# The first layer's key mask and key bias, added by VectorE and GpSimd instead of by row products on TensorE

## What is computed

```python
xn = _ln(x, ln_w, ln_b)
q = xn @ Wq + bq
k = xn @ Wk + bk + (1.0 - src_mask) * -1000000.0
q = softmax(q.reshape(b, t, h, dh), axis=-1)
k = softmax(k.reshape(b, t, h, dh), axis=1)      # over the 128 tokens
v = ((xn @ Wv + bv) * src_mask).reshape(b, t, h, dh)
att = einsum('bnhd,bnhl->bhdl', k, v)
y = einsum('bnhd,bhdl->bnhl', q, att).reshape(b, t, d)
scale, shift = split(silu(emb) @ W_emb + b_emb, 2)
hh = _ln(y, ln2_w, ln2_b) * (1.0 + scale) + shift
x = x + silu(hh) @ W_out + b_out
```

## Time and profile before

| | us |
|---|---|
| median of 3 runs | 2030.45 |
| the profiled execution | 2030.41 |
| its span, first to last instruction | 2028.6 |
| TensorE busy (granted clock 0.998) | 2002.7, 99% |
| VectorE busy | 1369.9, 68% |
| ScalarE busy | 1139.7, 56% |
| GpSimd busy | 573.2, 28% |
| one pair of layer 0, from 509.26 to the next pair's first key matmul at 537.75 | 28.49 |

### The profile page before, as it was taken

One profiled execution on the slowest core, in us unless ns is written; L12 is line 12 of the kernel. 1 busy time (PEld: TensorE's weight loads), 2 busy tenths in 40 slices (PEclk: granted clock), 3 DMA queues, 4 the chain that ended last, 5 costly groups with the idle time before them and its releaser, 6 DMA issues.

```text
span 2028.6 us, 52150 instructions
## 1 busy us (share of the span) xinstructions
PE 2002.7 (99%) x19499; PEld 1732.0 (85%) x19499; DVE 1369.9 (68%) x2995; ACT 1139.7 (56%) x3806; POOL 573.2 (28%) x861
## 2 busy tenths in 40 slices
PE   7999999999999999999999999999999999999997
PEld 5888888888888888888888888888888888888886
DVE  6877777777777777776666666666565656666665
ACT  4333343234333343244677777777777777777775
POOL 4233332333233332335222222222222222222220
PEclk9999999999999999999999999999999999999999
DMA  6311001110111001102110110101010101011000
GB/s 224 113 41 41 29 33 41 41 37 30 36 41 41 31 31 41 41 33 86 56 37 27 36 41 21 42 26 37 26 37 26 37 26 37 28 35 41 21 32 22
DMA packets 52165, 86.45 MB, mean 43 GB/s; under 512 B 5667, under 2 KB 14565, under 8 KB 52134
## 3 DMA queue, kind: packets, MB, share of 16 engines
q1 hardware_dynamic: 52118, 86.03, 12.5%
q10 hardware_dynamic: 16, 0.00, 0.0%
HBM read 52.32 MB, written 33.69 MB: 42 GB/s over the span
## 4 chain that ended last, share of the span: by engine, by line
PE 96%; DVE 2%; ACT 1%; DMA 0%; issue 0%; SPq 0%; POOL 0%; POOLq 0%; DVEq 0%; ACTq 0%
PE bank L538 16%; PE bank L540 14%; PE bank L539 14%; PE bank L547 9%; PE bank L548 9%; PE bank L549 9%; PE bank L559 7%; PE bank L1812 3%; PE bank L1787 3%; PE bank L1150 3%; PE bank L1136 2%; PE bank L1744 2%; PE bank L1781 1%; PE bank L1822 1%; PE bank L1038 1%; PE bank L1067 1%
## 5 line engine op out<-in xcount | busy, mean ns | idle before, releaser
L547 PE MATMUL bank<-xT_hi,w_hi 128*128 128x256 f32 x1536 | 448.9, 292 | 2.1 <-DVE xT_lo L379 1.4
L548 PE MATMUL bank<-xT_lo,w_hi 128*128 128x256 f32 x1536 | 438.8, 286 | 0.0
L549 PE MATMUL bank<-xT_hi,w_lo 128*128 128x256 f32 x1536 | 435.7, 284 | 0.0
L1598 ACT ACTIVATE heads<-bank,top 128x128 f32<-128x128 f32 x1024 | 359.2, 403 | 88.1 <-DVE top L1381 87.9
L538 PE MATMUL bank<-w_hi,xT_hi 128*128 128x512 f32 x768 | 306.3, 399 | 0.4 <-DVE bias_all L396 0.4
L547 PEld LDWEIGHTS bank<-xT_hi,w_hi 128*128 128x128 f32 x1536 | 291.9, 190 | 10.8 <-issue 5.1
L540 PE MATMUL bank<-w_lo,xT_hi 128*128 128x512 f32 x768 | 301.1, 392 | 0.0
L539 PE MATMUL bank<-w_hi,xT_lo 128*128 128x512 f32 x768 | 300.2, 391 | 0.0
L952 ACT ACTIVATE heads<-bank,k_neg 128x128 f32<-128x128 f32 x256 | 69.9, 377 | 404.4 <-DVE k_neg L814 404.4
L548 PEld LDWEIGHTS bank<-xT_lo,w_hi 128*128 128x128 f32 x1536 | 292.7, 191 | 0.5 <-issue 0.5
L549 PEld LDWEIGHTS bank<-xT_hi,w_lo 128*128 128x128 f32 x1536 | 292.9, 191 | 0.0
(11 more groups left out here) (204 smaller groups left out, 3730.8 us busy)
## 6 DMA issues: line engine op xcount, KB each, us to landing
xr<-in_x SPq DMA_DIRECT2D x32, 512.0 KB, 3.4
x_between_layers<-ends SPq DMA_DIRECT2D x64, 256.0 KB, 2.0
xr<-x_between_layers SPq DMA_DIRECT2D x32, 512.0 KB, 4.1
out<-ends SPq DMA_DIRECT2D x64, 256.0 KB, 2.1
store<-in_L_cond_W_emb SPq DMA_DIRECT2D x4, 1024.0 KB, 11.8
store<-in_L_cond_emb_w SPq DMA_DIRECT2D x3, 1024.0 KB, 8.2
mask_rows<-mask_parts SPq DMA_DIRECT2D x128, 2.0 KB
heads<-in_L_cond_Wk SPq DMA_DIRECT2D x1, 1024.0 KB, 7.8
```

What stands on the lines that cost most here:

```text
L547: yield nc.tensor.matmul(dst, w_hi[:, m, c, fs], a_hi[:, c], start=(first and c == 0), stop=False)
L548: yield nc.tensor.matmul(dst, w_hi[:, m, c, fs], a_lo[:, c], start=False, stop=False)
L549: yield nc.tensor.matmul(dst, w_lo[:, m, c, fs], a_hi[:, c], start=False, stop=(last and c == C - 1))
L1598: last = nc.scalar.activation(prob[:, a, c, :], ps[a][:, c * P:(c + 1) * P], ACT.Exp, bias=top[:, b, h:h + 1], accum_out=total[:, b, h:h + 1])
```

## The change

The mask (already times -1000000, less its largest value) is no longer split into parts for layer 0. It is written to memory and read back once per pair as a tile `key_mask` of 128 equal partitions, one slot, one pair ahead. VectorE adds it to the key block and takes the maximum in one operation per block of 128 x 128, with the sum written to `k_exp` and the maximum to `k_max`; each such operation is built as two instructions, the operation and a read of the accumulator. The key bias is left out of the exponent altogether, since it is constant along the tokens: GpSimd adds it to the maximum (`k_top`) and subtracts that from the bias (`k_neg`), and ScalarE takes the exponential of `k_exp` in place with `k_neg`. The bias is now four columns (`key_bias_cols`), made in the opening by four narrow matmuls and one addition. TensorE's row products are gone, and with them the tiles of rows, their four memsets and ScalarE's four small loads.

```diff
@@ first_steps, sync
+        sp.wait_ge(mask_step, 4)
+        sp.dma_start(mask_d[0, 0], mask_in[:, 0, :]).then_inc(mask_out, 16)
         sp.wait_ge(mask_step, 6)
         for n, part in enumerate((mask_hi, mask_lo)):
-            sp.dma_start(mask_d[:, n].rearrange("l b t -> b l t"), f32(part)).then_inc(mask_out, 16)
+            sp.dma_start(mask_d[1, n], f32(part[:, 1, :])).then_inc(parts_out, 16)
+        sp.wait_ge(mask_out, 16)
+        load_key_mask(sp, m, mask_d, 0, s["masks_in"])
         sp.wait_ge(x_in, 16)
         load_rows(sp, x_d, m.xr, 1, 1, x_in)
         emb.load(sp, range(4))
-        sp.wait_ge(mask_out, 32)
+        sp.wait_ge(parts_out, 32)
@@ first_steps, vector
-        nc.vector.tensor_tensor(m.key_row, ps[SUM_BANKS[0]][0:1, :], m.key_row, ALU.add).then_inc(key_step, 1)
-        dve.wait_ge(key_step, 1)
-        nc.vector.tensor_copy(key_bias[0:1, :], m.key_row).then_inc(key_step, 1)
-        dve.wait_ge(key_step, 2)
-        nc.vector.tensor_tensor(key_bias[32:33, :], m.key_row, f32(key_bias[0:1, :]),
-                                ALU.subtract).then_inc(s["key_bias"], 1)
+        r = vec_rows["L0_cond_bk"][0]
+        nc.vector.tensor_tensor(m.key_bias[:], ps[SUM_BANKS[0]][:, 0:C], m.vec[:, r:r + C],
+                                ALU.add).then_inc(s["key_bias"], 1)
@@ new
+def load_key_mask(sp, m, mask_d, pair, arrived):
+    sp.dma_start(m.key_mask[:], mask_d[0, 0, bass.ds(pair * PAIR, PAIR)].unsqueeze(0).broadcast_to([P, PAIR, P]))\
+        .then_inc(arrived, 16)
@@ layer0, sync
             if more:
+                sp.wait_ge(s["k_max"], seq(2, i, 2))
                 sp.wait_ge(x_in, seq(16, i, 32))
-                sp.wait_ge(s["masks_in"], seq(32, i, 64))
                 load_rows(sp, x_d, xr, i + 2, (i + 2) % RING, x_in)
-                load_masks(i + 2, (i + 2) % RING)
+                load_key_mask(sp, m, mask_d, i + 1, s["masks_in"])
@@ layer0, gpsimd (called between end(i - 1) and norm(i + 1))
+        def key_shift(pair):
+            for j in range(2):
+                some = slice(2 * j, 2 * j + 2)
+                bias = m.key_bias[:, some].unsqueeze(2).broadcast_to([P, 2, PAIR])
+                pool.wait_ge(s["k_max"], seq(2, pair, j + 1))
+                nc.gpsimd.tensor_tensor(k_top[:, some, :], k_max[:, some, :], bias, ALU.add).then_inc(s["k_top"], 1)
+                pool.wait_ge(s["k_top"], seq(2, pair, j + 1))
+                nc.gpsimd.tensor_tensor(k_neg[:, some, :], bias, k_top[:, some, :],
+                                        ALU.subtract).then_inc(s["k_neg"], 1)
@@ layer0, vector
         def key_maxima(i):
             for j in range(2):
+                if j == 0:
+                    dve.wait_ge(s["masks_in"], seq(16, i, 16))
                 dve.wait_ge(s["kT_ps"], seq(2, i, j + 1))
-                nc.vector.tensor_reduce(k_neg[:, 2 * j:2 * j + 2, :],
-                                        ps[j][:, :].rearrange("p (c b t) -> p c b t", c=2, b=PAIR), AX_X, ALU.max,
-                                        negate=True).then_inc(s["k_neg"], 1)
+                nc.vector.tensor_copy(m.keys_seen[:, j:j + 1], eps[:, 0:1])
+                for c in (2 * j, 2 * j + 1):
+                    for b in range(PAIR):
+                        at = (c - 2 * j) * PAIR * P + b * P
+                        last = nc.vector.tensor_tensor_reduce(k_exp[:, c, b, :], ps[j][:, at:at + P],
+                                                              m.key_mask[:, b, :], 1.0, LEAST, ALU.add, ALU.max,
+                                                              accum_out=k_max[:, c, b:b + 1])
+                last.then_inc(s["k_max"], 1)
@@ layer0, scalar, key_exps
-                        last = nc.scalar.activation(k_exp[:, c, b, :], ps[j][:, at:at + P], ACT.Exp,
+                        last = nc.scalar.activation(k_exp[:, c, b, :], k_exp[:, c, b, :], ACT.Exp,
                                                     bias=k_neg[:, c, b:b + 1])
@@ layer0, tensor
-            def key_biases(f):
-                dst = ps[f // 2][:, (f % 2) * PAIR * P:(f % 2 + 1) * PAIR * P]
-                done = nc.tensor.matmul(dst, key_bias[:, f * P:(f + 1) * P], mask_rows[:, i % RING, :],
-                                        start=False, stop=True)
```

More of the change, by code:

```diff
@@ L116, in build @@
         m.pairs = sb("pairs", [P, 2 * PAIR * (D + H0)])
-        m.rows = sb("rows", [P, D + RING * PAIR * P], F32R)
+        m.key_mask = sb("key_mask", [P, PAIR, P])
+        m.keys_seen = sb("keys_seen", [P, 2])
+        m.key_bias = sb("key_bias_cols", [P, C])
         m.v1 = sb("v1", [P, PAIR * D])
-        m.key_row = m.v_bias_flat[0:1, 4 * P:4 * P + D]
         m.mask_rows1 = sb("mask_rows1", [P, PAIR * P], F32R)
@@ L413, in total @@
             pe.wait_ge(part_out, k + 1)
+            if k == 0:
+                for f in range(C):
+                    last = nc.tensor.matmul(ps[SUM_BANKS[k]][:, f:f + 1], SPOTS[k][:, f * P:(f + 1) * P],
+                                            m.chunk_of[:, 0:1], start=True, stop=True)
+                last.then_inc(sum_ps, 1)
+                return
             nc.tensor.matmul(ps[SUM_BANKS[k]][:, :], m.chunk_of[:, 0:1].broadcast_to([P, P]), SPOTS[k], start=True,
@@ L626, in layer0 @@
     att = m.pairs[:, n:n + PAIR * C * DY].rearrange("p (b c d) -> p b c d", b=PAIR, c=C)
-    key_bias = m.rows[:, 0:D]
-    mask_rows = m.rows[:, D:].rearrange("p (r f) -> p r f", r=RING)
+    k_max = sb("k_max", [P, C, PAIR])
+    k_top = sb("k_top", [P, C, PAIR])
     k_neg = sb("k_neg", [P, C, PAIR])
@@ L646, in _ @@
         following = second["sync"](sp)
-        def load_masks(pair, slot):
-            for n, r in enumerate((64, 96)):
-                sp.dma_start(f32(mask_rows[r:r + 1, slot, :]),
-                             mask_d[0, n, bass.ds(pair * PAIR, PAIR)].rearrange("b t -> (b t)").unsqueeze(0))\
-                    .then_inc(s["masks_in"], 16)
         def store(prev):
@@ L664, in body @@
             if more:
+                sp.wait_ge(s["k_max"], seq(2, i, 2))
                 sp.wait_ge(x_in, seq(16, i, 32))
-                sp.wait_ge(s["masks_in"], seq(32, i, 64))
                 load_rows(sp, x_d, xr, i + 2, (i + 2) % RING, x_in)
-                load_masks(i + 2, (i + 2) % RING)
+                load_key_mask(sp, m, mask_d, i + 1, s["masks_in"])
+            elif not last:
+                sp.wait_ge(s["k_max"], seq(2, i, 2))
+                load_key_mask(sp, m, mask_d, i + 1, s["masks_in"])
+                next(following)
             else:
@@ L704, in end @@
             nc.gpsimd.tensor_copy(gains[:, 1], half_shift[:, 0, :, bass.ds(prev * PAIR, PAIR)]).then_inc(s["gains"], 1)
+        def key_shift(pair):
+            if isinstance(pair, int) and pair == 0:
+                pool.wait_ge(s["key_bias"], 2)
+            for j in range(2):
[6 more added lines that the diff above has]
+                                        ALU.subtract).then_inc(s["k_neg"], 1)
         def norm(pair):
```

61 lines of the change are left out of this document (21 added, 40 removed).

## The result

The changed kernel takes 2022.01 us (median of 6 runs, 2021.67 to 2025.42), the kernel before beside it 2030.47: a ratio of 0.9957 (95% interval 0.9947 to 0.9968). The gain is 8.5 us where 12.6 were forecast; the time lies in the range, faster by 0.42%. The execution whose profile is read first here took 2025.42 us (span 2023.5), the slowest of the six; a second profile of the same kernel (experiment 1) has 2021.07 us and a span of 2019.1.

What follows compares the result with a forecast made beforehand. TensorE's stream of matmuls, 28.49 us per pair, was taken to bound layer 0; 29 x 0.474 = 13.7, plus 0.1, plus 0.2, minus 1.4 made 12.6 us gained, 2030.41 to 2017.8 us, range 2015.5 to 2027.

Steps and rivals of the forecast that it cites:

- Removed from TensorE: Four row products per pair leave TensorE's stream, 0.1185 us each, 0.474 us per pair.
- the two end pairs: Pair 1, where TensorE waits 0.41 us, gains 0.1; the last pair, crowded with layer 1's first steps, gains 0.2.
- Added to VectorE: Eight fused additions with maximum and eight accumulator reads per pair: 0.28 us for both together, 2.39 us for a pair's maxima.
- The mask's load: A 128 KB tile behind x in SP's queue lands at 515.02 us and holds VectorE's maxima by 0.33 us.
- rival 1: The mask lands later, each 1 KB packet costing as much as 2 KB; TensorE waits in 29 pairs: 2023.3 us, 29%.
- Does TensorE notice?: At the last value matmul's weight load, the second query exponential still ends in time, with a margin of 0.23 us.
- Rival 2: On VectorE, reads don't overlap operations: 0.43 us instead of 0.28, TensorE short by 1.02 us per pair: 2047.4 us, 11%.
- The opening loses: SP waits for the mask's write before reading it back; first mask at 24.9 us, 1.4 us lost, bounds 0.9 and 2.4.
- Sum: Over the whole kernel, all terms together: 12.6 us gained, 2017.8 us.

Runs made afterwards that it cites:

- experiment 4: The kernel before with the row products left out from pair 1 on and nothing in their place: 2018.72 us, ratio 0.993.
- 8: The kernel before with each row product made twice from pair 1 on: 2048.74 us, ratio 1.0086.
- experiment 6: The changed kernel with eight more unused additions-with-maximum per pair on VectorE, behind the maxima: 2057.72 us, ratio 1.0128.
- experiment 5: The changed kernel with four more unused additions-with-maximum per pair on VectorE, behind the maxima: 2029.88 us, ratio 0.9997.
- 2: The changed kernel with pair 0's mask loaded straight from the input, not through memory and back: 2016.8 us, ratio 0.9922.
- 7: The changed kernel with pair 0's mask straight from the input and, in the loop, the mask issued ahead of x in SP's queue: 2017.93 us, ratio 0.9931.

## Why the prediction was right in kind and short in size

**Removed from TensorE: right in place, 9% too large.** Forecast 0.474 us per pair, measured 0.43. The step took the mean spacing of the stream with the rows in it; experiments 4 and 8 show that the spacing itself changes, so that one is worth 0.108. From pair 1 on that makes 13.2 us, where the step, the two end pairs included, had 14.0. The last pair gained 0.19, the 0.2 it was given. Pair 1 gained its full 0.43, not 0.1.

**Added to VectorE: the bounds missed.** 0.28 us for operation and read, bounds 0.26 to 0.43; measured 0.2125, below the lower one. The error lay in charging the read at all: on ScalarE it takes 0.09 us of the queue, on VectorE none. The Trainium skill, VectorE: DVE Perf Modes, section on the TRN2 errata, gave an estimate of 0.32, still further off; here the measurement decides.

**The mask's load: right in kind, and short.** In the pair read at first the hold is 0.36 us against 0.33, but that pair is a quiet one: the mean is 0.52. From issue to landing the forecast had 3.17 us (by bytes) and rival 1 3.59 (by packets); the median is 3.3, and single masks take 3.7, in other profiles 3.9. So the way by bytes is nearer, single masks come as late as rival 1 had them all, and its price, a wait of TensorE in each pair, did not come.

**Does TensorE notice? Hardly, and with more room than thought:** the load stands 0.69 us behind the exponential in the mean, against 0.23 forecast; 0.31 is the least in the first profile, 0.20, with the wait open, in the second. Two errors of the forecast have opposite signs here: the maxima are 0.55 us cheaper, and the mask comes 0.2 later in the mean. Rival 2 is out: no read waits for its operation's end. Its place and its kind of cost were right, as experiment 6 shows by opening the wait there; by the measured numbers a pair would lose what it gains where operation and read take 0.2125 + (0.60 + 0.43)/8 = 0.34 us, near the 0.36 that it named. Its sum has a slip: eight times 0.15 is 1.20 us and not 1.25, by which it would have been 0.97 per pair and 2045.9.

**The opening loses: the step that failed.** Forecast 1.4 us, bounds 0.9 and 2.4; measured 6.0, 4.4 and 6.7 in three profiles. Three things were wrong in it. The write was taken at the near end, "since it is now the first write and half as long"; it took 7.9 us, longer than all that the earlier trace rows show, and a write issued behind it landed before it, so its place in the queue gave it nothing. The read back was given 2.0 us, the time of a store in a quiet queue and named as the least; it took 3.3 to 4.8. And TensorE's idle time was priced at its length alone; in these three profiles 1.63 us at the lower clock came on top. What was right is that from the maxima to the value bias VectorE has no gap: that part takes 8.34 us after and 8.46 before, so each microsecond of the mask's delay arrives. In the first profile the loss adds up: 1.4 forecast, plus 1.2 for the write and 2.4 for the read (28.53 instead of 24.9), plus 1.6 for the clock, less 0.55 for cheaper maxima and 0.1 in the part behind them, 6.0.

**Sum.** In the second profile: 13.2 gained, 4.4 lost in the opening, 0.7 gained by scatter in layer 1, 9.5 in the span. In the first: 13.2, less 6.0, less 2.1 of scatter, 5.1. In the third: 13.0, less 6.7, plus 1.1, 7.4. The median's 8.5 lies among them. The forecast's 12.6 is off by 4: nearly 1 by the smaller price of the rows, the rest by the opening. That the result still lies in the range is partly luck: the upper end was set by rival 1, and not by an opening that loses 4 to 7 us.

## What to carry to other kernels

A change that takes a little out of each turn of a loop and puts a new dependence in front of it is paid for in the front as well, and here the front took a third to a half of what the loop gained: cost each step that runs once as carefully as the loop, and where data goes through memory and back behind full queues, add write, read and what stands still behind them. Such a detour is often avoidable: here the first tile could be made on the chip from the input while its engine was idle, worth 4 to 5 us more. And a way to learn a margin is to load the engine in steps until the wait opens, and to read it over all turns of the loop: one turn, here a quiet one, showed 0.2 us more room than the mean.

## What the runs showed of the hardware

- An accumulator read of VectorE starts together with the next operation and takes no time of its queue; the operation of 128 elements from a bank repeats at 0.2125 us, and the same from on-chip memory (L841) as well.
- Four equal matmuls are worth 0.43 us when taken away and 0.533 when added; the spacing of the others goes between 0.1185 and 0.120.
- Behind 2.6 to 3.7 us without work, TensorE ran eight matmuls of 512 columns 0.42 us apart (second profile, 38.61 to 41.99) between others at 0.23, in three profiles of three; kept busy before, it ran all of them at 0.23, in two of two. The eight make 1.5 us. Behind 2.82 us without work it ran all at 0.23 in experiment 5.
- Three small writes to memory, issued within 1.2 us behind full queues, did not land in the order of their issue: issued at 16.19, 16.75 and 17.39 us in the first profile of the change, they landed at 24.1, 22.4 and 24.4.
- In the opening the key matmuls of 256 columns can run 0.2125 us apart instead of 0.12, although the granted clock in those rows is 1.00, and for how long differs from one execution to another of the same kernel: for the first two blocks in the first profile of the change, for none in the second. Experiments 2 and 7 have the same opening, with one slow block and with two; TensorE from 20 to 25 us, the first row of 2, the second of 7:

```profile
20.00:25.00 5.00, 5.00 (x41) 1.00 1.07 360
```

```profile
20.00:25.00 5.00, 5.00 (x30) 1.00 1.07 362
```

It goes with a start of pair 1 at 53.98 and at 55.75, and in experiment 4, with one slow block, at 54.95 where three profiles with the same opening and none have 53.2 to 53.4. In the changed kernel it is hidden by the wait for the mask. What decides between the two was not tried.
